# Second mixture of experts: shared units first, routing beside them, x normed and turned between the first products, router in column groups

## The reference, cut to what matters

```python
x = x + tanh(g_ffn[1]) * _L1_ffn_ref(_layernorm(x), gate_w, Wg, Wu, Wd, sWg, sWu, sWd)

h = hidden_states.reshape(-1, 256)                       # 2048 tokens
shared = silu(h @ sWg) * (h @ sWu) @ sWd                 # 256 wide: two units of 128
routing_weights = sigmoid(h @ gate_w.T)                  # 16 experts
topk_w, topk_idx = top_k(routing_weights, 8)
topk_w = topk_w / (sum(topk_w) + 1e-06) * 2.5
comb[token, topk_idx] = topk_w
g, u = h @ Wg[e], h @ Wu[e]                              # each 256 -> 128
eo[e] = (silu(g) * u) @ Wd[e]                            # 128 -> 256
out = shared + sum over e of eo[e] * comb[:, e]
```

## Time and profile before

| | us |
|---|---|
| median of 3 runs | 2554.77 (2554.74 to 2556.43) |
| the profiled execution, its own time | 2553.6 |
| span of that execution | 2551.8 |
| TensorE busy | 2237.0 (88% of the span) |
| VectorE / ScalarE / GpSimd busy | 1829.5 / 1351.1 / 1250.5 |

### The profile page before, as it was taken

One profiled execution on the slowest core, in us unless ns is written; L12 is line 12 of the kernel. 1 busy time (PEld: TensorE's weight loads), 2 busy tenths in 40 slices (PEclk: granted clock), 3 DMA queues, 4 the chain that ended last, 5 costly groups with the idle time before them and its releaser, 6 DMA issues. The chain is left out here.

```text
span 2551.8 us, 47955 instructions
## 1 busy us (share of the span) xinstructions
PE 2237.0 (88%) x16834; PEld 1931.6 (76%) x16842; DVE 1829.5 (72%) x3739; ACT 1351.1 (53%) x3391; POOL 1250.5 (49%) x1701
## 2 busy tenths in 40 slices
PE   5969996799999989999985999978999993649996
PEld 2358885699999889999985888867888881327775
DVE  5866665699999898888884777764555547966775
ACT  1123333788888888888862333322444442436663
POOL 4904433799999788888871111112343441221112
PEclk9989998899999999999996999988999996768998
DMA  4201211200000110000003000010000000010001
GB/s 132 70 34 67 76 58 38 89 16 14 18 16 20 49 46 16 18 16 14 12 1 112 26 26 20 26 50 11 8 8 8 5 1 1 1 46 22 23 19 34
DMA packets 38652, 80.59 MB, mean 32 GB/s; under 512 B 5904, under 2 KB 25680, under 8 KB 34384
## 3 DMA queue, kind: packets, MB, share of 16 engines
q1 hardware_dynamic: 38416, 77.52, 9.1%
HBM read 64.92 MB, written 12.58 MB: 30 GB/s over the span
## 5 line engine op out<-in xcount | busy, mean ns | idle before, releaser
L1231 PE MATMUL bank<-l_wr,l_xq 128*128 128x128 f32 (+1 forms) x2048 | 272.5, 287 | 9.1 <-ACT l_raw L1340 8.0
L1231 PEld LDWEIGHTS bank<-l_wr,l_xq 128*128 128x128 f32 x2048 | 249.2, 194 | 10.1 <-issue 8.8
L793 PE MATMUL bank<-m_xr,m_wgr 128*128 128x512 f32 x864 | 211.2, 394 | 9.2 <-POOL m_wgr L853 9.2
L1354 ACT ACTIVATE xn_T<-bank,l_head_b,l_head_w 128x256 f32<-128x256 f32 x256 | 144.7, 565 | 118.8 <-PE bank L1278 118.8
L793 PEld LDWEIGHTS bank<-m_xr,m_wgr 128*128 128x128 f32 x864 | 159.1, 190 | 39.5 <-issue 9.2
L1568 POOL TENSOR_TENSOR l_tiny<-l_tiny,l_minus_half 128x6 f32<-128x6 f32 x128 | 175.8, 1374 | 10.7
L1267 PE MATMUL bank<-l_wpr,l_cat 128*128 128x256 f32 x1024 | 166.5, 305 | 1.9 <-POOL l_cat L1619 1.9
L1912 POOL TENSOR_TENSOR l_pr<-l_pr,l_rowsum 128x512 f32<-128x512 f32 x64 | 66.6, 1041 | 205.4 <-DVE l_rowsum L1879 205.4
L853 POOL TENSOR_TENSOR m_wgr<-m_wg,m_wgr 128x512 fp32r<-128x512 f32 x18 | 23.2, 1292 | 286.4 <-ACT m_wgr L831 286.4
L1619 POOL TENSOR_TENSOR l_cat<-l_yo,l_eo 128x512 fp32r<-128x512 bf16 x128 | 158.3, 1237 | 9.5 <-DVE l_yo L1443 8.2
L1494 DVE TENSOR_REDUCE l_rowsum<-xn_T 128x4 f32<-128x512 f32 x128 | 87.7, 686 | 100.9 <-ACT xn_T L1326 97.9
(11 more groups left out here) (320 smaller groups left out, 6408.5 us busy)
## 6 DMA issues: line engine op xcount, KB each, us to landing
l_stage<-in_l_w SPq DMA_DIRECT2D x8, 1024.0 KB, 4.9
l_centred<-l_stage SPq DMA_DIRECT2D x6, 1024.0 KB, 3.9
l_stage<-l_centred SPq DMA_DIRECT2D x6, 1024.0 KB, 4.8
m_unsplit<-in_m_w SPq DMA_DIRECT2D x14, 384.0 KB, 3.5
m_wg<-in_m_gu SPq DMA_DIRECT2D x18, 256.0 KB, 2.7
x_norm<-in_ctxT_b SPq DMA_DIRECT2D x32, 128.0 KB, 2.0
l_stage<-in_l_wp SPq DMA_DIRECT2D x4, 1024.0 KB, 5.0
l_saved<-l_xs SPq DMA_DIRECT2D x16, 256.0 KB, 2.0
```

Of the source, the lines that this page charges most:

```text
L793: r = e.matmul(banks[2 * (q % 2) + half][0:M, :], WGR[:, u % 2, a, k, sub, half, :], XR[:, b, k, cols], start=k == 0 and n == 0, stop=k == ...
L1231: e.matmul(bank[:, to:to + width], XQ[:, q % 2, v, k, :], WR[:, j, part, k, at:at + width], start=k == 0 and part == 0, stop=k == KT - 1 a ...
L1354: e.activation(tok(QT[:, n % 2, 3 * x:3 * x + 2, :]), ps[:, 0:2 * P], ACT.Identity, bias=head_b[:, 2 * x:2 * x + 1], scale=head_w[:, 2 * x ...
```

## The change

`moe` is replaced by `moe1`, written for this layer alone.

- The two shared units come first (the weight layouts are reordered), so steps 0 to 7 need no shares, only the gate. Their additions take the gate itself as factor.
- SyncE loads units 0 and 1 first, then the router, then the 13 weights of the next layer (`load_beside`), then units 2 to 17. ScalarE splits unit 0 ahead of the layer norm (`first_high`).
- The norm is not transposed by `layernorm`. VectorE norms blocks 0 to 7, GpSimd blocks 8 to 15. TensorE turns blocks 0 to 7 ahead of step 0 and 8 to 15 between the first products of steps 0 and 1. ScalarE copies each pair of blocks twice out of the bank, to `xn_T` and to the high part.
- The router is padded to 32 columns and stationary; blocks of x move past it, four of them into the four groups of 32 partitions of a bank. Two such calls (steps 0 and 1), two copies, four transposes and a copy (step 2) give the logits per token.
- The sigmoid is taken on ScalarE behind step 4, the eight largest on VectorE in its step 5, the marks in 6 and 7, the shares in 8.
- VectorE adds step n-2 to x in its step n, not n-1. The last four additions are each followed by the block statistics (`count`), and the next layer norm no longer takes them.
- Unit u is split ahead of the silu of step 4(u-1).

```diff
+            def raise_down(e, u):
+                e.wait_ge(*wd_in(u + 1))
+                if u >= 2:
+                    e.wait_ge(*down(4 * (u - 1)))
+                e.copy(WDR[:, u % 2, 0, :], WD[:, u % 2, :]).then_inc(wd_high.sem, 1)
...
+            def route_matmul(e, i, bank):
+                e.wait_ge(*kept(4 * (i + 1)))
...
+                for g in (2 * i, 2 * i + 1):
+                    for k in range(KT):
+                        for m in range(4):
+                            b = 4 * g + m
+                            r = e.matmul(bank[W * m:W * (m + 1), g * P:(g + 1) * P], router[:, k, :], XT[:, k, b * P:(b + 1) * P],
+                                         start=k == 0, stop=k == KT - 1)
...
             def tensor(e):
                 begin(e, ends)
...
+                turn(e, 0)
+                turn(e, 1)
+                for n in range(N + 1):
+                    if n == 1:
+                        turn(e, 2)
+                        turn(e, 3)
+                        e.wait_ge(*logits_in(1))
+                    if n < N:
+                        up_project(e, n)
+                    if n == 0:
+                        route_matmul(e, 0, banks[3])
+                    if n == 1:
+                        e.wait_ge(*xhi(8))
+                        route_matmul(e, 1, banks[6])
+                    if n == 2:
+                        turn_logits(e)
+                    if n >= 1:
+                        down_project(e, n - 1)
...
+                put_x(e, 0)
+                put_x(e, 1)
+                for n in range(N):
+                    u = n // 4 + 1
+                    if n % 4 == 0 and u < UNITS:
+                        raise_gu(e, u)
+                        raise_down(e, u)
+                    gate(e, n)
+                    if n == 0:
+                        keep_logits(e, 0, banks[3])
+                        put_x(e, 2)
+                    put_high(e, n)
+                    if n == 0:
+                        put_x(e, 3)
+                    if n == 1:
+                        keep_logits(e, 1, banks[6])
+                    if n == 2:
+                        keep_turned(e)
+                    if n == 4:
+                        e.wait_ge(*lturn_in(1))
+                        e.activation(pr[:, :, :], lg[:, :, :, 0:E].rearrange("p g m w -> p (g m) w"),
+                                     ACT.Sigmoid).then_inc(prob.sem, 1)
...
             def gpsimd(e):
                 begin(e, ends)
...
+                lower_gu(e, 0)
+                lower_down(e, 0)
+                e.wait_ge(*norm(B // 2))
+                for b in range(B // 2, B):
+                    normalise(e, b)
+                for u in range(1, UNITS):
+                    lower_gu(e, u)
+                    lower_down(e, u)
...
             def vector(e):
                 begin(e, ends)
...
+                for b in range(B // 2):
+                    normalise(e, b)
+                lower_x(e, 0)
+                lower_x(e, 1)
+                for n in range(N + 2):
+                    if 1 <= n <= N:
+                        lowest(e, n - 1)
+                    if n < N:
+                        hide(e, n)
+                    if n in (0, 1):
+                        lower_x(e, n + 2)
+                    if n >= 2:
+                        add(e, n - 2)
+                        if n - 2 >= N - 4:
+                            count(e, n - 2)
+                    if n == 5:
+                        route_top(e)
+                    if n in (6, 7):
+                        route_mark(e, n - 6)
+                    if n == 8:
+                        route_share(e)
```

More of the change, by code:

```diff
@@ L744, in moe @@
[L744 to L753, removed]
+            up = signals("up_projected", N)
@@ L754, in moe @@
+            silu = signals("silu", N)
+            hid = signals("hidden", N)
+            high = signals("moe_high", N)
+            low = signals("moe_low", N)
             down = signals("down_projected", N)
             acc = signals("moe_added", N)
[L757 to L769, removed]
+            bn = signals("x_counted", B)
@@ new lines, in turn @@
+            def turn(e, g):
+                for i in range(2):
+                    if g >= 2:
+                        e.wait_ge(*xhi(2 * (g - 2) + i + 1))
+                    for m in range(2):
+                        b = 4 * g + 2 * i + m
+                        e.wait_ge(*norm(b + 1))
+                        for k in range(KT):
+                            r = e.transpose(banks[4 + 2 * (g % 2) + i][:, (KT * m + k) * P:(KT * m + k + 1) * P],
+                                            xnorm[:, b % 4, k * P:(k + 1) * P], ident[:, :])
+                    r.then_inc(turned.sem, 1)
@@ L771, in tensor @@
             def tensor(e):
                 begin(e, ends)
[L773 to L809, removed]
@@ new lines, in put_x @@
+            def put_x(e, g):
+                for i in range(2):
+                    e.wait_ge(*turned(2 * g + i + 1))
+                    cols = slice((4 * g + 2 * i) * P, (4 * g + 2 * i + 2) * P)
+                    half = banks[4 + 2 * (g % 2) + i][:, :].rearrange("p (b k t) -> p k b t", b=2, k=KT)
+                    e.copy(XT[:, :, cols].rearrange("p k (b t) -> p k b t", b=2), half).then_inc(kept.sem, 1)
+                    e.copy(XR[:, 0, :, cols].rearrange("p k (b t) -> p k b t", b=2), half).then_inc(xhi.sem, 1)
@@ L818, in scalar @@
[L818 to L847, removed]
@@ new lines, in hide, with lowest @@
+            def hide(e, n):
+                e.wait_ge(*silu(n + 1))
+                if n >= 2:
+                    e.wait_ge(*low(n - 1))
+                e.tensor_tensor(HT[:, n % 2, :], SG[:, n % 2, :], banks[2 * (n % 2) + 1][:, :], ALU.mult).then_inc(hid.sem, 1)
+            def lowest(e, n):
+                e.wait_ge(*high(n + 1))
+                e.tensor_tensor(HBR[:, n % 2, 1, :], HT[:, n % 2, :], HBR[:, n % 2, 0, :].bitcast(F32),
+                                ALU.subtract).then_inc(low.sem, 1)
@@ L2457, in load @@
                     e.dma_start(t[(slice(0, parts),) + tuple(slice(None) for _ in shape[0][1:])], A[source]).then_inc(loaded.sem, 16)
+            if not begun:
+                return loaded, made, load
             stage(sync=load)
```

295 lines of the change are left out of this document (179 added, 116 removed).

## The result

The changed kernel takes 2572.65 us (median of 7 runs, 2563.45 to 2577.83), the kernel before on the same chip 2556.85 (7 runs, 2554.74 to 2563.22): a ratio of 1.0055 [1.0039, 1.0071]. It is slower by 14 us by the ratio (15.8 between the medians), not by 6. The profiled execution has a span of 2568.8 us and an own time of 2570.57, 17.0 over that of before.

The account below looks back on a forecast made before the run. TensorE was taken to bound the loop (busy 49.02 of 50 us), a chain of short works the head. Head -20.0, loop +23.0, routing +5.2 and tail -2.3 gave +5.9, about 2560.5 us; 80% range 2548 to 2569.

Parts of the forecast that it names:

- Part 1, the head: Norm to the first products of step 3: reordered, overlapped work saves 20.0 us (15 to 25).
- The cold step: Head: the first products of step 0 run at a lowered clock, taking 4.8 to 4.9 us.
- the third rival: Head shrinks less: GpSimd norms at 1.29 a block, turns wait over 4 us; +7, 2567.5 us; 15%.
- my 0.7: Head: the assumed GpSimd time to norm one block, 0.7 us, between 0.48 and 1.29.
- my lower bound of 1.7: Head: a routing call's least time, 0.05 us per record, if four groups run side by side; 2.9 was taken.
- Part 2, the loop's split: Loop: the split's wait delays silu and second products, 1.44 us for each of 16 units, +23.0.
- The rivals in which the silu is covered, in full or by half: Loop: full cover drops its term, 2537.5 us, 12%; half cover, with faster routing calls, centre 2552, 21%.
- Part 3, the routing: Loop steps 4 to 8: table loads, sigmoid, eight largest, marks and shares add 5.2 us (3.5 to 8).
- Part 4, the tail: Last first products to next norm: statistics taken in the loop save 2.3 us (1.5 to 3).
- the new order of additions: Loop: VectorE adding step n-2 removes a wait of 0.1 us that does not end last; worth nothing.
- its highest case: Head shrinks less than forecast, at 2567.5 us; 15%.

Follow-up runs that it names:

- e5: Changed kernel with all sixteen norms on VectorE and none on GpSimd: 2558.42 us, 0.9996 of the kernel before.
- e1: Changed kernel with the splits of units 2 to 17 back at their old place, ahead of the silu of step 4u-2: 2542.70 us, 0.9937.
- e3: Kernel before, with only the weight splits moved to the changed kernel's place: 2580.87 us, 1.0090.
- e8: Changed kernel, for units 2 to 17 the down half's split moved behind the high part of the same step: 2544.93 us, 0.9942.
- e4: Kernel before, with only the block statistics taken behind the last four additions in the loop: 2559.81 us, 1.0009.
- e11: e7 with all 16 block statistics taken by the next layer norm again, none in the loop: 2532.49 us, 0.9904.
- e2: Changed kernel run once more with no edit: 2569.91 us, 1.0051 of the kernel before.
- e9: Kernel before run once more with no edit: 2559.23 us, 0.9999.
- e7: Changed kernel with the edits of e1, e5 and e6 joined: 2530.16 us, 0.9889 of the kernel before.
- e6: Changed kernel with VectorE's routing work spread over steps 6 to 10, ahead of the step's own product: 2562.83 us, 1.0021.
- e10: Changed kernel with the edits of e8, e5 and e6 joined: 2529.03 us, 0.9883 of the kernel before.

## Why the prediction was right or wrong

**What failed.** The prediction gave the sum of the layer, +5.9, as the sum of the kernel. Every step ahead of and behind the layer stood in it at nothing, without a bound. The profiles show two misses, of 2.5 us in the layer and of 5 to 9 us outside it; the second is the larger, and it put the time above the range. A third, of 2.1, is in the base: I added to a median of 3 runs, 2554.77, and the median of 7 is 2556.85. With the layer's +8.4 on that base the time would be 2565.2, inside the range.

*Part 1, the head: -20.0 forecast, -20.3 measured, but by errors that cancel.* In us from the norm's first row:

| start of | forecast | measured |
|---|---|---|
| first products, step 0 | 12.3 | 11.8 |
| their length | 4.85 | 2.98 |
| routing call | 2.9 | 1.08 |
| first products, step 1 | 23.9 | 23.0 |
| their length | 2.9 | 5.18 |
| first products, step 2 | 31.1 | 30.7 |
| first products, step 3 | 38.1 | 37.7 |

The cold step is the second and not the first. GpSimd's norms of the second set took 6.12 / 4 = 1.53 each, near the value of the third rival and not my 0.7, so TensorE did little but short turns for 6 us ahead of step 1. The pairs of turns waited 1.03, 0.70, 2.15 and 0.45 for GpSimd, 4.3 together, over the 4 at which the third rival was to decide. Its mechanism was there; its price was paid for by the routing calls, 1.8 less each, and by step 0, 1.9 less. e5 shows what it costs: 7.3. That the errors cancel to 0.4 us at step 3 is luck, and so is a part of step 0: in e1 it was cold after all, and the head 2.4 longer.

The routing calls came out below my lower bound of 1.7. Each of the 32 records takes 1.08 / 32 = 0.034 us, against 1.09 / 8 = 0.136 for a full-width turn (the row at 1367.73). The Trainium skill's "TensorEngine Tiling (Array Packing)", section "Theoretical Speedup", gave up to four times; the trace agrees, 4.0. I had set its result beside the sum and not in it.

*Part 2, the loop's split: +23.0 forecast; +23.3 in e3, alone.* Wait, silu at 5.3, second products at 8.9 (1447.96 less 1439.08 = 8.88, forecast 8.86), unit in 18.77 (forecast 18.75): the chain is as written. e8 shows that the price is the queue behind the wait. The rivals in which the silu is covered, in full or by half, are refuted for this kernel.

*Part 3, the routing: +5.2 forecast, 7.7 in the changed kernel* (31.0 less 23.3): the mis-sized term of the layer. I had priced each delay at full clock. The row at 1410.59 has first products at 4.42 instead of 2.91, that at 1427.80 second products at 2.93 instead of 1.70: 2.7 more together, and without them the 7.7 would be 5.0. The granted clock around them, by stretch:

```profile
1411.00:1413.00 2.00, 2.00 (x6) 1.59 (x5) 1.87 (x18) 0.00 (x0) 0.00 (x0) 0.50 0.00 0
1427.80:1430.50 2.70, 2.70 (x12) 2.70 (x13) 2.70 (x6) 0.62 (x1) 0.00 (x0) 0.50 0.00 0
```

That is 1.2 GHz, in a loop that otherwise runs at 2.4 (granted 1.00, as in the stretch from 1500). Ahead of the first TensorE had idled 1.80 (1409.01), ahead of the second 3.62. With the splits at their old place (e1) the routing costs 298.3 - 293.7 = 4.6. There it has slow matmuls too, 1.6 us of them behind an idle of 1.84, but the idle of the shares' step is 1.00 and not 3.62, with no split in that step. e8 has no slow matmuls, and 3.6. So a stall in this loop can cost its own length and then again the slow matmuls behind it, and not every stall does: the sixteen of 1.20 have none (1.70 at 1447.96), nor has one of 1.78 in e5.

The rows of ScalarE around the sigmoid, in the changed kernel:

```profile
1401.22 1.28 ACT L948 ACT_TABLE_LOAD   x1
...
1402.52 0.41 ACT L948 ACTIVATE m_pr<-m_lg 128x256 f32<-128x256 f32 x1
...
1402.95 1.28 ACT L910 ACT_TABLE_LOAD   x1
1404.24 0.60 ACT L910 ACTIVATE m_sg<-bank 128x512 f32<-128x512 f32 x1
```

Each activation follows its load by 0.01 to 0.02 us, and the second load follows the sigmoid by 0.02. The Trainium skill's "ScalarE: Activation LUTs", section "What ACT_TABLE_LOAD costs", adds a drain of about 1.38 us to a switch; this trace does not agree, and here a switch is 1.28.

*Part 4, the tail: -2.3 forecast, -2.3 measured.* The sum was right and its reason half of it. The last second products start 7.95 behind the last first products (1722.32), forecast 7.97, but they take 1.70 and not 2.48. The forecast had the last additions wait for them, and they do not: VectorE is at the additions and statistics of the step before until 1725.19, a queue that the sum had left out. My own terms (2.48, 1.6 and 4 x 0.333 behind 1708.4) add up to 1713.8 and not to 1714.3, which is -2.8. I had also written that the new order of additions brings nothing. e4 shows that without it the statistics gain nothing; whether it has a part in the other 1.0 stays open (e11).

*Outside the layer: 0 forecast, +8.6 in the first pair of profiles, +5.2 in the second (e2 less e9).* By stages, most of it is in two. The attention of layer 2, next in line, takes 397.3 and 397.4 us in the two profiles of the changed kernel and 394.0 and 393.4 in the two of the kernel before. The same 20 us of that stage, from 30 us behind its norm's first row: first the kernel before,

```profile
1746.70:1756.70 10.00, 8.53 (x43) 7.95 (x42) 3.88 (x10) 0.00 (x0) 1.48 (x2) 0.56 0.00 1
1756.70:1766.70 10.00, 9.51 (x77) 8.66 (x75) 6.11 (x17) 4.76 (x20) 3.31 (x3) 1.00 0.05 15
```

then the changed one, where the clock stays low for longer and 55 matmuls stand for 77:

```profile
1758.30:1768.30 10.00, 8.53 (x38) 7.66 (x38) 3.30 (x7) 0.00 (x0) 2.13 (x2) 0.50 0.00 0
1768.30:1778.30 10.00, 10.00 (x55) 9.36 (x55) 4.47 (x13) 3.21 (x11) 0.85 (x2) 0.63 0.05 13
```

The other is the first mixture, long before the changed layer: 281.5 in the changed kernel's first profile, 278.8 and 278.7 in the two of the kernel before. But e2, the same program, has 278.7, and e4, which is the old program but for its tail, 280.9. Of the thirteen profiles four have 278.7 or 278.8 and nine 280.9 to 282.0, with kernels of both kinds in each group. In the first profile of the changed kernel one place there ran at half clock:

```profile
170.00:175.00 5.00, 5.00 (x13) 3.85 (x13) 3.00 (x5) 1.27 (x3) 0.00 (x0) 0.52 0.00 0
```

and in e2 it did not:

```profile
170.00:175.00 5.00, 5.00 (x30) 4.39 (x29) 3.70 (x7) 2.29 (x5) 0.00 (x0) 1.00 0.00 0
```

So the clock comes back some microseconds earlier or later in stages whose work is the same. The first mixture's share is then a matter of the execution and not of the change. The 3.3 to 4.0 in layer 2 repeats with the program, and it goes with the place of the splits more than with anything else: all six profiles with the splits at the old place have 393.1 to 394.0 (the two of the kernel before, e1, e4, e7, e11), and six of the seven with the new place have 396.2 to 397.4 (the two of the changed kernel, e3, e6, e8, e10). The seventh, e5, has 393.5. How the splits could reach it, the last of them some 40 us ahead of that stage, is open; no experiment here separated it from the moment at which the layer happens to begin.

In the medians the difference less that of the layer's profile is 15.8 - 8.4 = 7.4 us for the changed kernel, 3.6 for e2, 5.9 for e8 and 2.8 for e6. For all others it is within 2, e5 with -0.8, e1 and e3 close to nothing.

**The range.** It ended at 2569, its highest case being the head's. Two terms of 0 with 3 to 4 us either way, for two stages outside, would have reached the result. The side, slower, and the reason for it were right.

## What to carry to other kernels

Before moving a step that waits on an in-order queue, list what stands behind it and when the awaited work is issued: the same wait and copy cost 1.46 us a unit ahead of the silu and nothing to be measured behind the high part. When work is put into a loop that one engine bounds, put it where its engine already waits, and give a stall a case with slow matmuls behind it: here 2.7 us behind two of them, of 1.80 and 3.62. And give the untouched stages a bound of their own, from two executions of one kernel, before the sum of the changed part is called the sum of the kernel.

## What the runs showed of the hardware

- A norm of one block (128x256, two scalars for each partition) on GpSimd took 5.72 / 4 = 1.43 and 6.12 / 4 = 1.53 us; on VectorE a block is 0.39. With GpSimd's weight split beside it VectorE's six took 3.39, 0.57 each.
- A low part of 0.68 us on VectorE took 1.61 when GpSimd's 1.29 began 0.23 earlier (GpSimd from 1440.42, VectorE from 1440.65): it ended at 1442.26, 0.55 after GpSimd's end, so it had hardly moved until then.
- Matmuls with a stationary side of 32 columns ran at 0.034 us for each record of 128 columns, their weight loads with them.
